# Softmax row sums in a cross-attention kernel: five added pairs and three direct tiles in place of six pairs and one, and the group copies on VectorE in place of ScalarE

## What is computed

```python
q = (layernorm(x) @ Wq.T + bq)           # [4, 512, 16*32]
k, v = ctx @ Wk.T + bk, ctx @ Wv.T + bv  # [4, 1601, 16*32]
scores = clip(einsum('bhsd,bhtd->bhst', q, k) / sqrt(32), -50, 50)
scores = clip(where(mask, scores, -10000), -50, 50)
probs = softmax(scores)                  # over the 1601 tokens
ctx = einsum('bhst,bhtd->bhsd', probs, v)
```

## Time and profile before

| | us |
|---|---|
| median of 3 runs | 1665.86 |
| lowest and highest | 1662.44 and 1669.15 |
| profiled execution, its own time | 1663.85 |
| its span | 1661.8 |
| TensorE busy in the span | 1513.3 (91%) |
| VectorE busy | 960.2 (58%) |
| ScalarE busy | 744.2 (45%) |
| mean granted TensorE clock | 0.963 |

### The profile page before, as it was taken

One profiled execution on the slowest core, in us unless ns is written; L12 is line 12 of the kernel. 1 busy time (PEld: TensorE's weight loads), 2 busy tenths in 40 slices (PEclk: granted clock), 3 DMA queues, 4 the chain that ended last, 5 costly groups with the idle time before them and its releaser, 6 DMA issues. The chain is left out here.

```text
span 1661.8 us, 25708 instructions
## 1 busy us (share of the span) xinstructions
PE 1513.3 (91%) x10712; PEld 1021.2 (61%) x10712; DVE 960.2 (58%) x1459; ACT 744.2 (45%) x913; POOL 150.7 (9%) x163
## 2 busy tenths in 40 slices
PE   2563998998989998989998999988999999999998
PEld 2452773336863337943357843357788888888886
DVE  6631548994639983659965579947334243333333
ACT  1130438993249982459962379932222122121211
POOL 6666120001000001000000000010000000000000
PEclk9786998999999999989999999999999999999999
DMA  9464571005320005310033250044101011010001
GB/s 275 114 203 120 193 267 52 15 9 147 118 76 9 9 15 165 117 52 8 15 85 102 80 228 15 9 149 162 51 26 51 1 51 36 15 51 25 1 26 76
DMA packets 64164, 133.77 MB, mean 80 GB/s; under 512 B 22440, under 2 KB 42168, under 8 KB 58808
## 3 DMA queue, kind: packets, MB, share of 16 engines
q1 hardware_dynamic: 49048, 74.26, 13.4%
q0 software_dynamic: 15008, 57.97, 10.7%
HBM read 88.93 MB, written 43.25 MB: 80 GB/s over the span
## 5 line engine op out<-in xcount | busy, mean ns | idle before, releaser
L871 ACT ACTIVATE cx_probs<-cx_sc,proj_mbias 128x1024 f32<-128x1024 f32 (+1 forms) x416 | 442.7, 1114 | 40.5 <-PE cx_sc L1066 32.7
L987 DVE TENSOR_SCALAR cx_probs<-cx_probs 128x1024 f32<-128x1024 f32 (+1 forms) x416 | 270.6, 686 | 31.7 <-ACT cx_probs L871 30.2
L956 DVE TENSOR_TENSOR cx_padd<-cx_probs,cx_probs 128x1024 f32<-128x1024 f32 x192 | 234.1, 1219 | 0.8
L1066 PEld LDWEIGHTS cx_sc<-cx_q,cx_kt 32*128 32x128 f32 (+1 forms) x2496 | 103.4, 183 | 201.6 <-ACT cx_probs L871 187.2
L1079 PE MATMUL cx_acc<-cx_probs,cx_vt 128*32 128x512 f32 (+1 forms) x1664 | 221.6, 605 | 3.7 <-DVE cx_probs L987 3.7
L1066 PE MATMUL cx_sc<-cx_q,cx_kt 32*128 32x512 f32 (+1 forms) x2496 | 206.0, 432 | 17.8 <-ACT cx_probs L871 14.4
L136 PE MATMUL cx_sc<-proj_cs,proj_wk 128*128 128x256 f32 (+1 forms) x1344 | 173.7, 289 | 48.9 <-POOL cx_ones L755 40.2
L136 PEld LDWEIGHTS cx_sc<-proj_cs,proj_wk 128*128 128x128 f32 x1344 | 167.1, 195 | 57.6 <-POOL cx_ones L755 40.7
L136 PE MATMUL cx_sc<-proj_wv,proj_cs 128*128 128x512 f32 (+1 forms) x624 | 161.9, 416 | 4.6 <-DVE cx_kt L931 4.6
L136 PEld LDWEIGHTS cx_sc<-proj_wv,proj_cs 128*128 128x128 f32 (+1 forms) x624 | 118.2, 192 | 39.4 <-issue 10.2
L1091 PE MATMUL cx_tot<-cx_padd,cx_ones 128*32 128x256 f32 x1536 | 120.8, 390 | 0.0
(11 more groups left out here) (209 smaller groups left out, 1753.0 us busy)
## 6 DMA issues: line engine op xcount, KB each, us to landing
proj_raw<-in_ctxT SPq DMA_DIRECT2D x24, 512.0 KB, 3.7
scr_q<-qu_qs SPq DMA_DIRECT2D x4, 2048.0 KB, 6.6
scr_wd<-cx_wds POOLq DMA_DIRECT2D x16, 512.0 KB, 3.3
cx_q<-scr_q SPq DMA_DIRECT2D x4, 2048.0 KB, 9.2
cx_wo<-scr_wo POOLq DMA_DIRECT2D x3, 2048.0 KB, 13.5
scr_xs<-cx_xs POOLq DMA_DIRECT2D x3, 2048.0 KB, 6.8
qu_xt<-in_x SPq DMA_DIRECT2D x4, 1024.0 KB, 15.9
qu_fl<-in_wdT POOLq DMA_DIRECT2D x8, 512.0 KB, 7.3
```

What stands on the lines that cost most here:

```text
L871: nc.scalar.activation(prob(N)[0:r], sc[n % NSC][0:r], ACT.Exp, bias=mbias[0:r, b, t:t + 1], scale=SCALE).then_inc(exp_done, 1)
L956: nc.vector.tensor_tensor(padd[z][(g * QP + j) % 2][:], prob(2 * i + z)[:], prob(2 * i + 2 + z)[:], ALU.add).then_inc(added[z], 1)
L987: nc.vector.tensor_scalar(prob(N)[0:r], prob(N)[0:r], LOW, HIGH, ALU.max, ALU.min).then_inc(clip_done, 1)
L1066: last = nc.tensor.matmul(sc[(2 * i + h // 2) % NSC][0:r, h % 2], kt[own, z, c, t * P:t * P + r], q[own, y, c], start=n == 0, stop=n == 2)
```

## The change

Pairs go down from six to five (QP = TT // 2 - 1), so that tiles 0 to 9 are paired; tiles 10, 11 and 12 are summed directly by `single`, each in its own step. The count of contributions stays 13: 10 halves and 3 singles. Three halves are still owed to the next group. And `collect_values` and `collect_sums` move from ScalarE's instruction stream to VectorE's, at the same places of the loop (after the clip of tile 1, n = 0, and of tile 4, n = 0, and at the end of a sequence).

```diff
-    QP = TT // 2
-    SUMS = 2 * QP + 1
+    QP = TT // 2 - 1
+    LONE = 2 * QP
+    OWED = 3
+    SUMS = 2 * QP + TT - LONE
...
         def sums_until(g, j):
-            return g * SUMS + 2 * j + 2 + (1 if j >= QP - 2 else 0)
+            half = 2 * j + 1
+            return g * SUMS + half + 1 + (TT - LONE if half >= LONE - OWED else 0)
...
                 def exps(b):
...
-                            if ot < TT - 1:
+                            if ot < LONE:
                                 act.wait_ge(added[n % 2], og * QP + ot // 2 + 1)
                             else:
-                                act.wait_ge(sums_done, og * SUMS + SINGLE)
+                                act.wait_ge(sums_done, og * SUMS + LONE - OWED + ot - LONE + 1)
...
-                        if c and n % 2 == 0 and t == 1:
-                            collect_values(b, c - 1)
-                        if c and n % 2 == 0 and t == 4:
-                            collect_sums(b, c - 1)
-                    collect_values(b, HC - 1)
-                    collect_sums(b, HC - 1)
...
+                def collect_values(b, c):
+                    g = b * HC + c
+                    dve.wait_ge(values_done, (g + 1) * TT)
+                    at_least(dve, stored, g * STORES * 16)
+                    nc.vector.tensor_copy(ob[:], acc[:]).then_inc(acc_out, 1)
+
+                def collect_sums(b, c):
+                    g = b * HC + c
+                    dve.wait_ge(sums_done, (g + 1) * SUMS)
+                    at_least(dve, stored, g * STORES * 16)
+                    nc.vector.tensor_copy(os[:], tot[:]).then_inc(tot_out, 1)
...
                 def clips(b):
...
-                        if t % 2 and n % 2:
+                        if t % 2 and t < LONE and n % 2:
                             add(b, c, t // 2, 0)
-                        if t and t % 2 == 0 and n % 2:
+                        if t and t % 2 == 0 and t <= LONE and n % 2:
                             add(b, c, t // 2 - 1, 1)
+                        if c and n % 2 == 0 and t == 1:
+                            collect_values(b, c - 1)
+                        if c and n % 2 == 0 and t == 4:
+                            collect_sums(b, c - 1)
...
+                    collect_values(b, HC - 1)
+                    collect_sums(b, HC - 1)
...
-                def single(b, c):
-                    N = (b * STEPS + (c + 1) * TT - 1) * 2
+                def single(b, c, t):
+
+                    N, r = (b * STEPS + c * TT + t) * 2, rows_of(t)
...
                 def weigh(b, i):
                     c, t = divmod(i, TT)
-                    if t < 3 and c:
+                    if t < OWED and c:
                         owed(b, c - 1, t)
-                    if 3 <= t < TT - 1:
-                        sums(b, c, (t - 3) // 2, (t - 3) % 2)
+                    if OWED <= t < LONE:
+                        sums(b, c, (t - OWED) // 2, (t - OWED) % 2)
                     values(b, i)
-                    if t == TT - 1:
-                        single(b, c)
+                    if t >= LONE:
+                        single(b, c, t)
```

More of the change, by code:

```diff
@@ L697, in sums_until @@
         def sums_until(g, j):
-            return g * SUMS + 2 * j + 2 + (1 if j >= QP - 2 else 0)
-        SINGLE = 2 * QP - 2
+            half = 2 * j + 1
+            return g * SUMS + half + 1 + (TT - LONE if half >= LONE - OWED else 0)
         def prob(N):
@@ L843, in values_out @@
                             down_hi(p, "first values")
[L845 to L855, removed]
                 def exps(b):
@@ L1093, in sums @@
                     last.then_inc(sums_done, 1)
-                def single(b, c):
-                    N = (b * STEPS + (c + 1) * TT - 1) * 2
+                def single(b, c, t):
+                    N, r = (b * STEPS + c * TT + t) * 2, rows_of(t)
                     for h in range(HC):
-                        last = nc.tensor.matmul(tot[h * HD:(h + 1) * HD], ones[0:TLAST], prob(N + h // 2)[0:TLAST, h % 2],
+                        last = nc.tensor.matmul(tot[h * HD:(h + 1) * HD], ones[0:r], prob(N + h // 2)[0:r, h % 2],
                                                 start=False, stop=False)
@@ L1103, in weigh @@
                     c, t = divmod(i, TT)
-                    if t < 3 and c:
+                    if t < OWED and c:
                         owed(b, c - 1, t)
-                    if 3 <= t < TT - 1:
-                        sums(b, c, (t - 3) // 2, (t - 3) % 2)
+                    if OWED <= t < LONE:
+                        sums(b, c, (t - OWED) // 2, (t - OWED) % 2)
                     values(b, i)
-                    if t == TT - 1:
-                        single(b, c)
+                    if t >= LONE:
+                        single(b, c, t)
                 def owed(b, c, n):
-                    sums(b, c, QP - 2 + (n + 1) // 2, (n + 1) % 2)
+                    half = LONE - OWED + n
+                    sums(b, c, half // 2, half % 2)
                 pe.wait_ge(pads, 1)
@@ L1149, in _ @@
                     weigh(b, STEPS - 1)
-                    for n in range(3):
+                    for n in range(OWED):
                         owed(b, HC - 1, n)
```

## The result

| | before | changed |
|---|---|---|
| median, us | 1666.71 (4 runs) | 1686.22 (4 runs) |
| lowest and highest | 1662.44 and 1669.15 | 1684.35 and 1693.03 |
| profiled execution, its own time | 1663.85 | 1684.35 |
| its span | 1661.8 | 1682.1 |

The ratio of the runs is 1.0127, 95% interval 1.0092 to 1.0163: slower by 21 us. Between the two profiled executions the span grew by 20.3 us. The forecast was 1685, which is +21.0 us on 1663.85.

A forecast was written before the change was run, and what follows sets the result against it. The prediction took TensorE, running through its own stream, to bound the kernel. Its terms, +10.3 - 0.8 + 11.5 = +21.0 us on the profiled 1663.85 us, gave 1684.9, rounded to 1685 us; range 1677 to 1690.

The forecast's parts named there:

- What bounds: Attention steps: TensorE, running through its own stream, sets the pace at 2.32 us a normal step; VectorE is very near.
- Sums on TensorE: Tiles 10 and 11: singles replace halves, 0.86 us more a group, 12 groups followed by another: +10.3 us.
- End of a sequence: Last tile's values no longer wait for VectorE behind an add: -0.2 us, 4 times, -0.8 us.
- Adds taken off: VectorE, tiles 11, 12 and following: 2 x 1.13 us less a group, gaining nothing.
- Copy of the values: acc to ob on VectorE behind tile 1's clip, n = 0: costs nothing, 0.6 us to spare.
- Copy of the sums: tot to os on VectorE behind tile 4's clip, n = 0: TensorE 0.96 us late, 12 times, +11.5 us.
- The price without it: Copy of tot priced at the SBUF copy's 418 ns: stall 0.69 us, 8.3 us in all.
- Copies taken off ScalarE: ScalarE: 2 x about 0.5 us less a group, gaining nothing since it follows TensorE.
- first rival: Before a group's first half of sums: no stall at tot, only the sums cost, +9.5, 1673.4 us; chance 0.11.
- second: Attention groups: VectorE sets the pace, its relief counts, -1.06 us a group, 1647 us; chance 0.04.
- third: Behind the 12 stalls: pauses cost TensorE clock as well, 1.4 us each, +17 on top, 1702 us; chance 0.05.
- the late clip: VectorE, tile 4, n = 0: exp ends 567.09, clip begins 567.80; harmless before, since values lag scores by two steps.

The follow-up runs named there:

- e1: Kernel before with five pairs and three direct tiles, both copies left on ScalarE; ratio to the kernel before 1.0058.
- e7: Kernel before with four pairs and five singles, both copies left on ScalarE; ratio to the kernel before 1.0159.
- e6: Changed kernel with the copy of the sums back on ScalarE, that of the values on VectorE; ratio to the kernel before 1.0053.
- e8: Changed kernel with the copy of the values later, behind tile 1's second clip, in front of the add; ratio to the kernel before 1.0132.
- e4: Changed kernel with the copy of the sums later, behind tile 4's second clip and the following add; ratio to the kernel before 1.0253.
- e3: Changed kernel with the copy of the sums earlier, behind tile 3's second clip, in front of the add; ratio to the kernel before 1.0087.
- e5: Kernel before, six pairs, both copies on VectorE, that of the sums behind tile 3's second clip, before the add; ratio to the kernel before 1.0021.

## Why the prediction was right, point by point

- *What bounds:* right. TensorE through its own stream; e1 and e7 show it without a microsecond of idle time while VectorE gets lighter.
- *Sums on TensorE:* +10.3 predicted for 12 groups. The steps are 2.70, 2.76 and 2.75 us where 2.33, 2.33 (2.28 before a 65-token step) and 2.75 stood. In attention time e1 gives 9.15 us, of which the end of a sequence takes back 4 x 0.28, so the groups cost 10.3 (12 x 0.86).
- *End of a sequence:* -0.8 predicted, 4 x (5.17 - 5.45) = -1.1 measured. The six places of 0.87 us were really 5.17 in sum.
- *Adds taken off:* nothing, as predicted: VectorE starts the group early and is back in step at the add of 568.39, which waits for the owed half. One sign of being wrong was exps that wait for adds: the kernel before has 8 such waits (2.9 us in all), the changed kernel none.
- *Copy of the values:* nothing (e6), with 0.6 us of cover (e8).
- *Copy of the sums:* 12 x 0.96 = 11.5 predicted. The copy took 683 ns where 685 was taken from a two-operand row, the gap was 0.89 us and the step grew by 0.93; changed minus e1 is 11.2 us. The row that gave the price was a weaker ground than the prediction says, and that it hit to 2 ns is partly luck: VectorE's two-operand adds of the same size with both operands in SBUF took a median of 684 and 686 ns in the same trace (L285), so that row doesn't tell the PSUM source from the second operand. The rule of the Trainium skill that was weighed there, in "VectorE: DVE Perf Modes", section "Why PSUM operands drop a tier", agrees: 683 ns from PSUM against 418 ns from SBUF for the same 128x512. The price without it, 8.3 us, was too low.
- *Copies taken off ScalarE:* nothing, as predicted; its idle time before exps that wait for scores rose from 32.7 to 72.7 us.
- *Rivals:* the gap did appear (first rival out); lighter VectorE bought nothing (second out). In the changed kernel the granted clock stayed at 1.00 in the stretch shown, and all 12 steps with a gap took 3.27 to 3.29 us, so no gap of 0.9 us cost clock (third out). Behind one gap of 2.62 us it did happen (e4).

The sum by rows was +21.0; measured were +20.3 in the span, +20.3 in attention time and +19.5 between the medians (1686.22 - 1666.71). Term by term it is 10.3 - 1.1 + 11.2 against 10.3 - 0.8 + 11.5. What the prediction understated is how full VectorE is: it allowed the late clip as harmless before, which it was, but a place 0.6 us later for an add costs 0.2 us (e3).

## What to carry to other kernels

In a pipeline of engines that run nearly in step, look for the engine whose stream repeats at fixed distances while its releasers end at varying ones; work added there counts in full, and work taken from the others counts for nothing. Moving an instruction to a less busy engine is a question of the place in that engine's queue: write down when the operands of everything ahead of it are ready, when the consumer wants the result, and compare with the length; here the same copy cost 11.2 us behind one clip, 2.4 us in front of the add before it, 32 us one clip and one add later (and 1.5 us of clock), and nothing on the engine that ran ahead. A stretch between two marks inside the bound engine's stream, repeated in each pass, tells a microsecond where timed runs tell ten.

## What I had not expected of the hardware

Apart from the first sequence of e4, the stretches of attention repeat to 0.05 us between the sequences of an execution, and between executions too (e1 and e6, two kernels with one copy on different engines, agree in their sum of 460.5), while timed executions of the same kernel spread by 19 us (before, 1657.17 to 1676.54 in 23 runs). So the profiles give no sign that the spread is made in the attention groups: what the span has beyond the attention time goes from 1205.9 (e1) to 1215.8 us (e5) over the ten profiled kernels. Where it is made I haven't tested. The first steps of a sequence, which took 1.65 us for scores at their start, vary by up to 1.8 us (13.9 to 15.7 us from the first scores of the third sequence to its first half of sums). And of the 23 runs the shortest had a mean granted clock of 0.968 and the longest 0.957; whether the clock makes the difference or only goes with it, no run here separates.
